# Two decoder layers on one core: the order of both projections, the queue of their operand loads, and where the router weights are loaded

## What is computed

```
# layer 0, attention: 16 heads of 8
q, k, v = (norm(x) @ W.T for W in (q_heads, k_heads, v_heads))
x += softmax(causal(q @ k.T / sqrt(8))) @ v @ output_proj.T
# layer 0, experts: a shared one and 2 of 8
probs = softmax(norm(x) @ Wr); gate = the two largest, scaled to a sum of 1
x += mlp(shared) + sum(gate[e] * mlp(e))            # gelu, 512 hidden
# layer 1, attention: 16 heads of 64, keys and values from 32 latent columns
latent = norm(x) @ Wkv_down
k, v = latent @ Wk_up, latent @ Wv_up;  q = norm(x) @ Wq
x += softmax(causal(q @ k.T / 8)) @ v @ Wout
# layer 1, experts: a shared one and 8 of 16, sigmoid scores, silu(gate) * up, down
```

## Time and profile before

| | us |
|---|---|
| median of 3 runs (2308.87 to 2311.86) | 2310.61 |
| the profiled execution | 2308.57 |
| its span in the profile (1.67 less) | 2306.9 |
| PE busy / DVE / ACT / POOL | 2088.4 / 1535.3 / 1387.6 / 467.9 |
| first projection, until attention begins | 0 to 82.9 |
| attention and output projection of layer 0 | 82.9 to 663.2 |
| weights, statistics, router of layer 0 | 663.2 to 727.4 |
| experts of layer 0 | 727.4 to 1136.6 |
| statistics and second projection | 1136.6 to 1218.5 |
| attention and output projection of layer 1 | 1218.5 to 1940.6 |
| weights, statistics, router of layer 1 | 1940.6 to 2009.5 |
| experts of layer 1 | 2009.5 to 2306.9 |

### The profile page before, as it was taken

One profiled execution on the slowest core, in us unless ns is written; L12 is line 12 of the kernel. 1 busy time (PEld: TensorE's weight loads), 2 busy tenths in 40 slices (PEclk: granted clock), 3 DMA queues, 4 the chain that ended last, 5 costly groups with the idle time before them and its releaser, 6 DMA issues. The chain is left out here.

```text
span 2306.9 us, 43330 instructions
## 1 busy us (share of the span) xinstructions
PE 2088.4 (91%) x10730; PEld 1347.7 (58%) x10732; DVE 1535.3 (67%) x6217; ACT 1387.6 (60%) x2517; POOL 467.9 (20%) x803
## 2 busy tenths in 40 slices
PE   4499999999956999999878999999999997399998
PEld 3355555555455888888634555555555557378886
DVE  6578777777445777777656666666666634477776
ACT  5066666666645999999643555555555564355554
POOL 2011111111112000000000111111111110276666
PEclk9599999999976999999997999999999998599999
DMA  5323333334132112112086455554455511175762
GB/s 175 119 39 55 49 51 57 50 49 58 18 105 40 37 37 55 37 36 55 35 284 138 116 116 130 130 125 115 116 122 130 130 24 59 38 155 114 139 119 60
DMA packets 99755, 202.83 MB, mean 88 GB/s; under 512 B 14528, under 2 KB 36288, under 8 KB 99136
## 3 DMA queue, kind: packets, MB, share of 16 engines
q1 hardware_dynamic: 99648, 201.65, 38.9%
HBM read 169.47 MB, written 31.60 MB: 87 GB/s over the span
## 5 line engine op out<-in xcount | busy, mean ns | idle before, releaser
L667 DVE CUSTOM_DVE_ANT_0 a1ms<-a1S,mask_q 128x128 bf16<-128x128 f32 (+1 forms) x758 | 387.8, 553 | 184.1 <-issue 180.7
L721 ACT ACTIVATE a1p<-a1T 128x512 f32<-128x512 f32 x576 | 331.4, 597 | 294.4 <-PE a1T L823 293.9
L667 DVE CUSTOM_DVE_ANT_0 a0ms<-a0S,mask_q 128x384 bf16<-128x384 f32 (+2 forms) x752 | 379.6, 553 | 111.1 <-issue 84.0
L721 ACT ACTIVATE a0p<-a0T 128x512 f32<-128x512 f32 x576 | 330.4, 597 | 182.6 <-PE a0T L823 171.6
L802 PE MATMUL a1O<-a1p,a1v 128*33 128x512 f32 (+3 forms) x1536 | 304.6, 496 | 1.0 <-POOL a1p L635 0.9
L823 PE MATMUL a0T<-a0qT,a0kT 128*128 128x512 f32 (+3 forms) x768 | 265.8, 393 | 12.1 <-ACT a0p L721 6.5
L1282 DVE TENSOR_TENSOR m_hl<-m_h,m_hh 128x512 fp32r<-128x512 f32 x288 | 197.7, 690 | 115.4 <-ACT m_hh L1238 110.4
L823 PE MATMUL a1T<-a1qT,a1kT 97*128 97x512 f32 (+3 forms) x768 | 263.1, 390 | 0.6 <-DMA a1qT<-a1mr 0.6
L762 PE MATMUL a0S<-a0kS,a0qS 128*128 128x384 f32 (+2 forms) x752 | 229.2, 361 | 32.7 <-PEq L283 25.4
L823 PEld LDWEIGHTS a1T<-a1qT,a1kT 97*128 97x128 f32 x768 | 131.8, 189 | 200.8 <-ACT a1p L721 144.5
L762 PE MATMUL a1S<-a1kS,a1qS 96*128 96x128 f32 (+1 forms) x758 | 220.7, 353 | 13.8 <-DMA a1kS<-scr_k 13.6
(11 more groups left out here) (245 smaller groups left out, 3604.5 us busy)
## 6 DMA issues: line engine op xcount, KB each, us to landing
m_gb<-scr_g SPq DMA_DIRECT2D x48, 1024.0 KB, 8.4
a1qS<-scr_q SPq DMA_DIRECT2D x96, 256.0 KB, 6.1
a1qT<-scr_q SPq DMA_DIRECT2D x96, 256.0 KB, 4.0
a1kS<-scr_k SPq DMA_DIRECT2D x96, 128.0 KB, 6.8
a1kT<-scr_k SPq DMA_DIRECT2D x96, 128.0 KB, 4.7
scr_q<-p_hi SPq DMA_DIRECT2D x32, 256.0 KB, 2.3
scr_q<-p_lo SPq DMA_DIRECT2D x32, 256.0 KB, 2.5
a0qS<-scr_q SPq DMA_DIRECT2D x48, 128.0 KB
```

The source lines that it names most:

```text
L667: nc.vector.tensor_tensor_reduce(masked_s[spare][:, 0:c1 - c0], buf[:, 0:c1 - c0], k.mask_q[:, SEQ - w + c0:SEQ - w + c1], 1.0, NEVER, ALU ...
L721: nc.scalar.activation(prob_of(g, p)[:, h, :], t_ps[slot % 2][:, :], ACT.Exp, scale=scale)\
```

## The change

1. `in_turn` takes a distance `ahead`. VectorE normalises two supertiles ahead of the low parts in both projections; the other engines keep a distance of one. `project_1` is now written out in this form, without registers.
2. The operand loads of the first two groups are issued by ScalarE, in `project_0` after its copies of supertiles 3, 4, 5 and 7, with the waits that stood before them on SP. `project_1` does the same, and `load_all` goes.
3. `project_1` has a ring of five slots, three of them in the tile of attention's result, and a v of its own for all supertiles. It no longer waits for its stores: attention does, on SP, before its next loads.
4. POOL clears two of the eight operand tiles (`qS0`, `kS0`), VectorE `kS1`, ScalarE the two `kT` and `qS1`. The two `qT` are filled by DMA on SP's queue from the zeros of the mask, in pieces of 1 KB.
5. The weights of both routers and the bias are loaded in `project_0`; `load_ahead` goes, and `route` issues the expert weights itself.
6. `stats_chain` loses a link: the root takes scale and `eps`. Halving the mean and the copy of the two largest become operations with two inputs.

```diff
-def in_turn(n, front, back):
-
-    front(0)
-    for s in range(n):
-        if s + 1 < n:
-            front(s + 1)
-        back(s)
+def in_turn(n, front, back, ahead=1):
+
+    for s in range(n + ahead):
+        if s < n:
+            front(s)
+        if s >= ahead:
+            back(s - ahead)
...
-    nc.vector.tensor_scalar(k.mean[:, :], k.mean[:, :], 0.5, None, ALU.mult).then_inc(combined, 1)
+    nc.vector.scalar_tensor_tensor(k.mean[:, :], k.mean[:, :], 0.5, k.mask_q[:, 0:TILES], ALU.mult, ALU.add).then_inc(combined, 1)
...
-    link(nc.vector.tensor_scalar(k.rstd[:, :], k.rstd[:, :], 1.0 / D, EPS, ALU.mult, ALU.add))
...
-            nc.scalar.activation(k.rstd[:, :], k.rstd[:, :], ACT.Sqrt).then_inc(std_ready, 1)
+            nc.scalar.activation(k.rstd[:, :], k.rstd[:, :], ACT.Sqrt, scale=1.0 / D, bias=k.eps[:, :]).then_inc(std_ready, 1)
...
-        by_pool = [operands.qS[0], operands.kS[0], operands.qS[1], operands.kS[1]]
-        FILLS = 4
+        by_pool = [operands.qS[0], operands.kS[0]]
+        FILLS = 4 + 2 * 16
...
+                sp.wait_ge(made, 4)
+                for t in operands.qT:
+                    sp.dma_start(t[:, :, :].bitcast(F32).rearrange("p h (a n) -> p (h a) n", n=ST // 2),
+                                 k.mask_q[:, 0:ST].bitcast(F32).unsqueeze(1).broadcast_to([P, 16, ST // 2])).then_inc(filled, 16)
...
-                nc.vector.memset(operands.qT[1][:, :, :].bitcast(F32), 0.0).then_inc(filled, 1)
+                nc.vector.memset(operands.kS[1][:, :, :].bitcast(F32), 0.0).then_inc(filled, 1)
...
-                in_turn(NST, front, back)
+                in_turn(NST, front, back, 2)
...
+                    if s == 3:
+
+                        act.wait_ge(filled, FILLS)
+                        act.wait_ge(ones_set, VDEPTH + len(by_pool))
+                        act.wait_ge(*stores(0))
+                        act.wait_ge(*stores(1))
+                        operands.load_S(act, (0, 0))
+                    elif s == 4:
+
+                        act.wait_ge(*v_stores(0))
+                        act.wait_ge(*v_stores(1))
+                        operands.load_T(act, (0, 0))
+                    elif s == 5:
+                        operands.load_S(act, (0, 1))
...
                 in_turn(NST, front, back)
+                operands.load_T(act, (0, 1))
...
-def route(k, name, E, K, w_router, bias_row, xh, xl, gate_rows, weights, weights_loaded, absorb=None):
+def route(k, name, E, K, wr, bias, xh, xl, gate_rows, weights, sources, absorb=None):
...
-                sp.dma_start(wr[:, :], w_router).then_inc(loaded, 16)
-                if bias_row is not None:
-                    sp.dma_start(bias[:, :], bias_row.partition_broadcast(P)).then_inc(loaded, 16)
+                for (raw, _, _), source in zip(weights, sources):
+                    sp.dma_start(raw, source).then_inc(weights_loaded, 16)
...
-                    link(nc.vector.tensor_copy(top[:, :, 0:K], srt[:, :, 0:K]))
+                    link(nc.vector.tensor_tensor(top[:, :, 0:K], srt[:, :, 0:K], srt[:, :, 0:K], ALU.max))
...
-                for par in range(2):
-                    sp.wait_ge(stored[par], 16 * NSTORE * (NST // 2))
...
-                pipelined(dve, NST // 2, front, back)
+                in_turn(NST, front, back, 2)
...
+                    if s == 3:
+
+                        act.wait_ge(*stores(0))
+                        act.wait_ge(*stores(1))
+                        operands.load_S(act, (0, 0))
+                    elif s == 4:
+                        operands.load_T(act, (0, 0))
+                    elif s == 5:
+                        operands.load_S(act, (0, 1))
...
+        return [stores(s) for s in range(NST - DEPTH, NST)]
...
+        k.routers_loaded = k.sem("w_r_ld"), 16 * 3
...
+            for dst, src in ((router[0], a["L0_ffn_Wr"]), (router[1], a["L1_ffn_gate_w"]),
+                             (bias, a["L1_ffn_expert_bias"].partition_broadcast(P))):
+                sp.dma_start(dst[:, :], src).then_inc(k.routers_loaded[0], 16)
...
-                attention(k, "a1", 2, 32, 64.0 ** -0.5, rows, attn, load_all(rows))
+                spare = [flat[:, n * 2560 + 1024:n * 2560 + 3584].bitcast(F32R).rearrange("p (n c) -> p n c", c=ST) for n in range(6)]
+                own = [[sb(c1, f"p1_{n}{i}", [P, 5, ST], F32R)[:, :, :] for n in ("hi", "lo")] for i in range(2)]
+                v_rows = sb(c1, "p1_v1", [P, TILES, 33])
+                stores = project_1(k, a_q, a["L1_attn_Wkv_down"], q1, k1, v1, rows, own + [spare[0:2], spare[2:4], spare[4:6]], v_rows)
+
+                attention(k, "a1", 2, 32, 64.0 ** -0.5, rows, attn, None, wait_stored(stores))
```

More of the change, by code:

```diff
@@ L334, in _ @@
                                         base=0, pattern=[[-1, P]], channel_multiplier=1).then_inc(made, 1)
+                nc.gpsimd.memset(k.eps[:, :], EPS).then_inc(made, 1)
                 for t in v1:
@@ L1342, in project_1 @@
     NT = NC + 1
+    DEPTH = len(ring)
     with ExitStack() as c:
@@ L1357, in project_1, with stores @@
         loaded, LOADED = k.params_loaded(1)
-        stored = [sem(f"p1_st{i}") for i in range(2)]
+        stored = [sem(f"p1_st{i}") for i in range(DEPTH)]
         NSTORE = 2 * NT + 1
         rows = [P] * NC + [LD]
+        def stores(s):
+            return stored[s % DEPTH], 16 * NSTORE * (s // DEPTH + 1)
         with nc.Block() as block:
@@ L1392, in _, with front, back @@
             def _(dve):
-                def front(g):
-                    wait_past(dve, xT_done, lin(g, 1, -1))
-                    normalise(k, dve, xn[g[1]], g, xn_ready)
-                def back(g):
-                    u, par = g
-                    wait_past(dve, stored[par], u * (16 * NSTORE))
+                def front(s):
+                    if s >= 2:
+                        dve.wait_ge(xT_done, s - 1)
+                    normalise(k, dve, xn[s % 2], (0, s), xn_ready)
+                def back(s):
+                    if s >= DEPTH:
+                        dve.wait_ge(*stores(s - DEPTH))
+                    hi, lo = ring[s % DEPTH]
@@ L1420, in back @@
+                def back(s):
+                    if s >= DEPTH:
+                        act.wait_ge(*stores(s - DEPTH))
+                    hi, _ = ring[s % DEPTH]
                     for n in range(NT):
[L1421 to L1424 removed]
+                        act.wait_ge(t_done, s * NT + n + 1)
+                        nc.scalar.copy(hi[0:rows[n], n, :], t_ps[n][0:rows[n], :]).then_inc(hi_ready, 1)
+                    act.wait_ge(v_done, s + 1)
+                    nc.scalar.copy(v1[:, s * TPS:(s + 1) * TPS, 0:LD], v_ps[:, 0:TPS * LD].rearrange("p (t c) -> p t c", t=TPS))\
@@ L1430, in _, with front @@
+                act.wait_ge(prepared, 1)
+                in_turn(NST, front, back)
+                operands.load_T(act, (0, 1))
             @block.tensor
             def _(pe):
-                def front(g):
-                    par = g[1]
-                    pe.wait_ge(xn_ready, lin(g, 1, 1))
+                def front(s):
+                    pe.wait_ge(xn_ready, s + 1)
                     for t in range(TPS):
-                        last = nc.tensor.transpose(xT_ps[par][:, t * P:(t + 1) * P], xn[par][:, t, :], k.ident[:, :])
+                        last = nc.tensor.transpose(xT_ps[s % 2][:, t * P:(t + 1) * P], xn[s % 2][:, t, :], k.ident[:, :])
@@ L1454, in _ @@
                 pe.wait_ge(loaded, LOADED)
-                pipelined(pe, NST // 2, front, back)
+                in_turn(NST, front, back)
+        return [stores(s) for s in range(NST - DEPTH, NST)]
 def moe_1(k, wg, wu, wd, xh, xl, gate_rows, out):
@@ L1767, in transformer @@
                 parts = [[t[:, :, :] for t in (r, *x)] for r, x in zip(raw, w)]
-                w_loaded = load_ahead(k, "w1_ld", [x[0] for x in parts], [a[n] for n in ("w_gate", "w_up", "w_down")])
+                sources = [a[n] for n in ("w_gate", "w_up", "w_down")]
                 ln_stats(k)
-                route(k, "r1", 16, 8, a["L1_ffn_gate_w"], a["L1_ffn_expert_bias"], xh, xl, gate_rows1, parts, w_loaded)
+                route(k, "r1", 16, 8, router[1], bias, xh, xl, gate_rows1, parts, sources)
             moe_1(k, *w, xh, xl, gate_rows1, out)
-def load_ahead(k, name, tiles, sources):
-    loaded = k.sem(name)
-    with k.nc.Block() as block:
-        @block.sync
-        def _(sp):
-            for tile, source in zip(tiles, sources):
-                sp.dma_start(tile, source).then_inc(loaded, 16)
-    return loaded
 def kernel(**inputs):
```

117 lines of the change are left out of this document (45 added, 72 removed).

## The result

| | before | after |
|---|---|---|
| median of 4 runs, us | 2309.74 (2305.57 to 2311.86) | 2283.68 (2282.72 to 2290.23) |
| ratio, 95% interval | | 0.9895 [0.9872, 0.9919] |
| the profiled execution, its span | 2308.57, 2306.9 | 2290.23, 2288.4 |
| first attention matmul of layer 0 | 82.91 | 86.81 |
| attention and output projection of layer 0 | 580.3 | 585.2 |

The change saves 26 us of the 36.5 forecast. The profiled execution is the longest of the four by 6 us. Its attention of layer 0, which the change doesn't touch, took 4.9 us longer than before.

The account below looks back on a forecast made before the run. Time could come only from 298 us of projections and routers, with transfers setting the projections' end. Savings 11.0 + 8.0 + 0.2 + 7.3 + 10 = 36.5 us from 2308.57 gave 2272.1, or 2274.1 from the median; forecast 2273, range 2260 to 2290.

Parts of the forecast that it names:

- Routers: Both routers: no separate weights' block, no TensorE wait for router weights, a shorter statistics chain; 11.0 and 8.0 us saved.
- The maximum: Routers: the copy turned into a two-input maximum still waits beside POOL's subtraction, so it gains 0.
- The start: Kernel start: with two POOL memsets fewer, normalising begins at 15.6 instead of 19.34, 3.8 us earlier.
- Second projection: Layer 1's projection: attention begins earlier without waiting for stores to land; gain between 4.5 and 13, taken as 10 us.
- First projection: Layer 0's projection: earlier start and moved loads less the fills' price; gain 4.3 to 10.3, taken as 7.3 us.
- so 48 to 54: First projection: us the engine half serving loads and stores needs, instead of 56.5; upper end if moved loads compete with stores.
- The fills' 2 us: First projection: 2 us charged for the short packets of the DMA fills made before the stores.
- A: Transfers bind everywhere: first projection loses 5, second gains 4.5 us, 18.7 saved in all, 2290 us; chance 0.20.
- Rival B: Routers: the two-input maximum doesn't wait for POOL, giving 2.4 and 3.4 us more, 2270 us; chance 0.12.
- C: Projections: DMA engines used in full and SP never held, gains 15 and 13, 2261 to 2262 us; chance 0.10.
- D: Projections: 52 issues moved to ScalarE stop its copies; slower from 1.63 us an issue, 2329 us at 2.02; chance 0.03.
- over 1 us each: Projections: sign that the forecast is wrong, ScalarE's load issues taking more than 1 us apiece.

Follow-up runs that it names:

- pool_fills: Changed kernel with the two qT tiles cleared by POOL's memsets instead of filled by DMA: 2280.34 us, ratio 0.9886 to the kernel before.
- wait_p1: Changed kernel with SP again waiting at the second projection's end until all stores have landed: 2292.87 us, ratio 0.9937 to the kernel before.
- sp_loads_p1: Changed kernel with the second projection's operand loads issued on SP's queue between the stores: 2290.05 us, ratio 0.9914 to the kernel before.
- sp_loads_p0: Changed kernel with the first projection's operand loads back on SP's queue, fills still by DMA: 2278.57 us, ratio 0.9872 to the kernel before.

## Why the prediction was right, and where not

The time, 2283.68, lies in the range and on the side that was forecast, 10.7 us above the number. In the profile the first projection alone is 11.2 us off its term (3.9 lost where 7.3 were to be gained), and the other stages together 2.2.

- **Routers: right**, a little under the number. Forecast 11.0 and 8.0, measured 64.3 - 54.6 = 9.7 and 68.9 - 61.3 = 7.6. TensorE's wait for the router's weights is gone and the expert weights had cover. The 0.2 us for the shorter statistics chain didn't come: from its first row to the normalising it took 2.57 us where it took 2.48, because ScalarE's table load and root (1.28 and 0.32) are the longer side; the root with scale and `eps` in it takes 0.32 where it took 0.23.
- **The maximum: right**, 2.62 us beside POOL's subtraction where the copy took 2.59. By this row the rule on operations with two SBUF inputs and a GpSimd operation that reads SBUF (the Trainium skill, "SBUF — State Buffer", section "SBUF: two separate sides") holds here. The same sentence of that section names operations in a two-port mode, which wait for any GpSimd operation. The normalising, with one input, waited beside a memset (pool_fills), which fits; in which mode it ran, no row shows.
- **The start: right**, 3.65 us for 3.8, in spite of a misread row: the 5.64 us of `mean*0.5` end at 18.11, with POOL's fourth memset (18.07), not with the third. With two memsets fewer both are gone.
- **Second projection: the size right, the reasons half.** Forecast 10, measured 81.8 - 72.1 = 9.7 for the first scores and 10.6 for the second. Not waiting for the stores to land is worth 7 (wait_p1), and the loads on ScalarE 4.3 (sp_loads_p1). The order, which was counted as six waits of 1.4 us that make room, gave 3 to 5. The five slots, said to keep ScalarE from waiting for its ring, did so, and two began attention 3 us earlier. These prices are each from one profile and don't add up to the 9.7. That 10 was so near is partly luck: it was picked between 13, if SP is never held, and 4.5, if it is held to the last tile. SP was held, until 14 us behind TensorE's end.
- **First projection: wrong.** The term is "so 48 to 54", the time that the transfers take on the half of the engines that serves stores and loads, and both ends of it were too small. The step from 48 to 54 is the price of moving the loads to ScalarE's queue, 0 to 6 us, of which the forecast took 3; the move cost 8.4 (86.0 against 77.6 in sp_loads_p0). The sum of bytes over rates had no place for who waits meanwhile: a v store landed after 14.3 us instead of 6 to 7, ScalarE waited 17.8 us in all for the ring of three v tiles with the last loads behind those waits in its own stream, and the block's end waits for the last v store to land. The 48 itself holds for loads behind the last store, as on SP's queue, and would put attention at 72.6 (the forecast 75.6 less 3). Measured without the move is 77.6, so 5 us more: from the first store at 22.2 to attention went by 55.4 us, with the engines 83% busy, and not 48. Of the 5.3 us gained there against 82.9, 3.65 are the start. TensorE's last product ended at 43.7 in that run, so it isn't what binds; how much is rate and how much is waiting for the v ring stays open.
- The fills' 2 us: at 77.6 in both forms with the loads on SP the price is 0; with the loads on ScalarE one profile says 4. That their short packets cost anything, no run shows.

Of the rivals, A was right for the first projection (loss of 5 forecast, 3.1 to 3.9 measured against the one profile before, though two of the seven profiles show none) and wrong for the second (gain of 4.5 forecast, 9.7 measured). By the sentence cited with it (the Trainium skill, "DMA: Bandwidth & Descriptors", section "Issuing engines are not separate DMA queues"), a second issuing engine only saves issuing time. Here the same move lost 8.4 us in the first projection and gained 4.3 in the second. The Trainium skill, "DMA: Bandwidth & Descriptors", section "Queues, rings and completion order", says that a DMA engine takes turns between the queues for which it has work; by that rule a load on a second queue delays a store that is under way, where on one queue it would stand behind it. The landing times agree (14.3 us against 6.9), but no row shows the turns themselves.

Rival B fell with the 2.62 us; its time was also added up wrongly, since 2.4 and 3.4 us more would have given 2266, not 2270. C fell because the engines were not used in full (77% from 22.0 to 86.4 us) and SP was held. D needed 1.63 us for an issue; ScalarE's 52 took 28.95 us in the profile, 0.56 each, with six at 1.0 to 1.2 where the queue was full. The sign "over 1 us each" was thus seen in six issues, and ScalarE's copies did stand still behind them, but the mean is far from D's.

## What to carry to other kernels

Moving loads to a second engine's queue doesn't only spare issue time: it reorders transfers. Where a later step waits for a store to land (a short ring, a block's end), try it with nothing beside that store; where the block ends with the last issue, as in the second projection here, a second issuing engine pays.

Before making the transfers at a stage's end faster, ask which of them the next stage's first step needs. The largest gains of this study, 11.8 us in the first projection and 10.8 in the second by the medians, moved no byte less: they let scores begin while stores that these don't need were still going out.

A deeper ring kept the engine that fills it from waiting, and attention began no earlier for it: try the shallow one as well.

## What the hardware showed that was not expected

- The same instructions with loads and stores on two queues began attention at 82.7 to 90.0 us in seven profiles; with both on SP's queue, at 77.6 in two profiles. A 288 KB store landed after 11.9 to 15.2 us in the seven, and after 6.9 and 7.0 in the two.
- A VectorE operation with two tiles as input ran 0.19 us beside a memset of POOL, while one with one tile as input waited: eight normalisings took 4.05 us instead of 2.13.
- The share of the DMA engines doesn't tell what they move: at 1.04 to 1.05 they moved 229 GB/s with loads alone, 349 with loads 4.29 of 11.17 MB, and 387 with loads 1.82 of 9.28 MB.
